# A graph network kernel: the opening stage's edge loads in rows of 112, 15 and 1, node scores laced with the normalisation, weight loads moved back

## What is computed

```python
h = jnp.maximum(_layernorm(x, axis=-1), 0.0)              # per node
hh = jnp.einsum('ni,hio->nho', h, W_att)
e = (hh[src] * a_src).sum(-1) + (hh[dst] * a_dst).sum(-1)  # 4 scores per edge
for _ in range(2):                                         # two hops of means
    h = segment_sum(h[src], dst) / deg
```

## Time and profile before

| what | us |
|---|---|
| median of 3 runs | 5965.78 |
| lowest and highest | 5952.73, 5968.33 |
| the profiled execution, its own time | 5961.54 |
| span of that execution | 5959.8 |
| busy: PE, DVE, POOL, ACT | 4565.7, 5147.9, 4326.5, 1746.8 |

### The profile page before, as it was taken

The page is one execution under the profiler, slowest core; times in us unless marked ns, Lnnn a source line. Parts: engine busy times, 40 slices in busy tenths (PEclk is TensorE's granted clock), DMA queues, the critical chain, the costliest instruction groups (busy, mean ns, idle before and its releaser), DMA issues. The chain is left out here.

```text
span 5959.8 us, 120870 instructions
## 1 busy us (share of the span) xinstructions
PE 4565.7 (77%) x44915; PEld 4261.9 (72%) x44915; DVE 5147.9 (86%) x13477; ACT 1746.8 (29%) x3789; POOL 4326.5 (73%) x4429
## 2 busy tenths in 40 slices
PE   5887773444434489999799997999979999799996
PEld 4776762222222379899799987999979999699996
DVE  6987776777777679999799997999979999799997
ACT  1111113767666522222122221222212222122221
POOL 4777778777777647777677776777767777677776
PEclk9999885665565689999799997999979999799998
DMA  3444443888888724444244442444424444344442
GB/s 90 123 117 117 117 111 109 299 292 293 291 290 291 249 75 117 116 114 116 74 118 114 117 113 76 117 114 115 116 73 119 115 116 114 80 112 115 115 116 79
DMA packets 514218, 827.78 MB, mean 139 GB/s; under 512 B 115666, under 2 KB 222043, under 8 KB 500577
## 3 DMA queue, kind: packets, MB, share of 16 engines
q1 hardware_dynamic: 372656, 645.16, 31.7%
q0 software_dynamic: 140976, 174.89, 16.4%
HBM read 385.20 MB, written 434.48 MB: 138 GB/s over the span
## 5 line engine op out<-in xcount | busy, mean ns | idle before, releaser
L663 POOL DMA_INDIRECT gring<-tableh,src_i x2778 | 2658.6, 957 | 997.3 <-issue 732.0
L1241 PE MATMUL psum<-penalty,arena 125*128 125x192 bf16 x25240 | 2309.1, 247 | 235.4 <-DVE es_w L1644 120.7
L1241 PEld LDWEIGHTS psum<-penalty,arena 125*128 125x128 bf16 x25240 | 2111.8, 98 | 277.8 <-issue 271.6
L663 POOL DMA_INDIRECT gring<-table,src_i x1414 | 1446.6, 1023 | 492.3 <-issue 406.3
L1644 DVE TENSOR_SCALAR arena<-dst_f,node_id 125x640 bf16<-125x640 f16 x5060 | 1746.6, 397 | 0.1
L898 ACT COPY run<-by_lane 128x512 f32<-128x512 f32 x505 | 570.1, 1129 | 2744.6 <-DVE by_lane L1706 2744.6
L1706 DVE TENSOR_TENSOR_SCAN by_lane<-mask_x,psum 128x256 f32<-128x256 f32 x1010 | 630.5, 663 | 0.2
L1579 DVE SCALAR_TENSOR_TENSOR arena<-arena,mask 128x324 f32<-128x324 f32 x808 | 444.3, 550 | 170.9 <-ACT arena L835 170.0
L1016 PE MATMUL psum<-ident,by_lane 128*128 128x128 f32 x202 | 66.6, 433 | 659.0 <-DMA by_lane<-attr_last 595.7
L1258 PEld LDWEIGHTS psum<-arena 128*128 128x128 f32 x4040 | 535.8, 193 | 14.4
L1016 PEld LDWEIGHTS psum<-ident,by_lane 128*128 128x128 f32 x202 | 29.2, 203 | 718.2 <-issue 718.2
(11 more groups left out here) (256 smaller groups left out, 4808.7 us busy)
## 6 DMA issues: line engine op xcount, KB each, us to landing
rows<-arena SPq DMA_DIRECT2D x101, 1296.0 KB, 5.1
acts<-arena SPq DMA_DIRECT2D x505, 256.0 KB, 2.1
arena<-acts SPq DMA_DIRECT2D x505, 256.0 KB
rowsg<-run SPq DMA_DIRECT2D x505, 256.0 KB
gring<-tableh,src_i POOLq DMA_INDIRECT x2778
rows<-run SPq DMA_DIRECT2D x101, 256.0 KB, 2.0
dst_f<-pe_src SPq DMA_DIRECT2D x253, 93.8 KB
gring<-table,src_i POOLq DMA_INDIRECT x1414
```

Source lines behind the costliest of these rows:

```text
L663: pool.indirect_dma_start(ring[:, s, k, :], None, table, bass.IndirectOffsetOnAxis(ap=src_i[:, c * K + k:c * K + k + 1], axis=0))\
L1241: ins = mm(found(n)[:, m, :], hot_at(n // 2, j)[:, at:at + P], parts[:, j, :, :].rearrange("q a f -> q (a f)"), start=(j == 0), stop=(j == ...
```

## The change

- The edge numbers are loaded as rows 0 to 111, rows 112 to 126 and the last row, three DMAs for each of `src_i` and `dst_i` (`edges_in` goes from 96 to 128).
- SP's fills of `ed_edges`, `rows*` and `attr_last` and its loads of `e1_hop`, `e1_gat` and `be1_c` move ahead of the table stores. The loads of `weights_in` move behind the first two `load_cols1` and `load_nat`.
- ACT laces the five square roots with the copies of the scores. The transposed group has two buffers (`hT2`: `hT` and the first 64 partitions of `yp`). PE transposes group g+1 ahead of the scores of group g; the transposes of `src_cols` stand before group 4's transposes.
- DVE's split of `t1` waits for the scores of its group instead of for the stored table, and the `pen_m` part stands between groups 3 and 4 of the split.
- The split of `be_rows` moves from ahead of chunk 0 into chunk 54; ACT doesn't wait for `weights_in` any more.
- `hT` is allocated ahead of `run1`, so the tiles between its two places lie at other addresses.

```diff
             for to, of in ((src_i, src), (dst_i, dst)):
-                sp.dma_start(to[0:P - 1, :], of[0:(P - 1) * T].rearrange("(p t) -> p t", p=P - 1))\
-                    .then_inc(edges_in, 16)
+                most = of[0:(P - 1) * T].rearrange("(p t) -> p t", p=P - 1)
+                for lo, hi in ((0, P - 16), (P - 16, P - 1)):
+                    sp.dma_start(to[lo:hi, :], most[lo:hi, :]).then_inc(edges_in, 16)
...
+        hT2 = (hT[:, :, :], yp[0:F, :, :])
...
+            ln_root(0)
             act.wait_ge(v_T, 1)
             copy(wattT[:, :, :], psum[0:F, 0, 0:H * F].rearrange("p (h i) -> p h i", h=H)).then_inc(v_Tsb, 1)
+            ln_root(1)
             act.wait_ge(v_ps, 1)
             copy(vvec[:, :], psum[0:F, 1, 0:2 * H]).then_inc(v_sb, 1)
+            copy_h0(0)
+            ln_root(2)
+            copy_h0(1)
+            ln_root(3)
+            copy_scores(0)
+            ln_root(4)
+            copy_h0(2)
+            copy_scores(1)
+            copy_h0(3)
+            copy_scores(2)
+            act.wait_ge(src_T_ps, 1)
...
+            copy_h0(4)
+            copy_scores(3)
+            copy_scores(4)
...
-            act.wait_ge(weights_in, N_WEIGHTS * 16)
...
             for g in range(NG):
-                if g == NG - 1:
+                if g == 3:
                     pe.wait_ge(src_cols_set, 1)
...
                 pe.wait_ge(h0_Tsb, g + 1)
+                if g + 1 < NG:
+                    pe.wait_ge(h0_ready, g + 2)
+                    transpose_group(t1[:, grp(g + 1), 0:F], 2, h0_T)
                 if g:
                     pe.wait_ge(es_sb, 2 * g)
                 for k in range(GJ):
-                    ins = mm(psum[0:NQ, 1, 64 + k * 2 * H:64 + (k + 1) * 2 * H], hT[:, k, :], vvec[:, :],
+                    ins = mm(psum[0:NQ, 1, 64 + k * 2 * H:64 + (k + 1) * 2 * H], hT2[g % 2][:, k, :], vvec[:, :],
                              start=True, stop=True)
                 ins.then_inc(es_ps, 1)
-                if g + 1 < NG:
-                    pe.wait_ge(h0_ready, g + 2)
-                    transpose_group(t1[:, grp(g + 1), 0:F], 2, h0_T)
...
+                    if k == 0 and c == 2 * NJ + 4:
+                        split_be()
...
-            dve.wait_ge(t1_out, NG * 16)
-            dve.wait_ge(t2h_ready, 1)
-            for g in range(NG):
+            def split1(g):
+
+                dve.wait_ge(es_sb, 2 * g + 2)
...
+            for g in range(NG - 1):
+                split1(g)
+            dve.wait_ge(bc_ready, 1)
...
+            split1(NG - 1)
+            dve.wait_ge(t1_out, NG * 16)
+            dve.wait_ge(t2h_ready, 1)
             dve.wait_ge(ed_zeroed, 96)
             dve.wait_ge(heads_set, 2)
             rows_from(0)
             rows_between(0)
             one_hot1(0, 0, NJ)
             one_hot1(1, 0, NJ // 2)
-            dve.wait_ge(weights_in, N_WEIGHTS * 16)
-            be = Steps(dve, be_steps)
...
```

More of the change, by code:

```diff
@@ L207, in part @@
             return stage[:, used[0] - width:used[0]]
+        hT = sb("hT", [F, GJ, NQ])
         act_in = part(SL * 4 * P).rearrange("p (s n) -> p s n", s=SL)
@@ L270, in build @@
         fold_b = sb("fold_b", [1, F])
-        hT = sb("hT", [F, GJ, NQ])
         xT = sb("xT", [P, 3, NQ])
@@ L454, in _ @@
             sp.dma_start(attr_last[0:LAST, :], attr[(P - 1) * T:E, :]).then_inc(attr_padded, 16)
[L456 to L469, removed]
             sp.wait_ge(e1_zero, 2)
@@ L480, in _ @@
                     sp.dma_start(be1_c[q * F:(q + 1) * F, :], be1.rearrange("l d -> d l")).then_inc(e1_in, 16)
+            for g in range(NG):
+                if g == NG - 1:
+                    sp.wait_ge(src_T_sb, 1)
+                    for i in range(3):
+                        rows = min(P, PE_COLS - i * P)
+                        sp.dma_start(pe_src[i * P:i * P + rows, :], src_T[0:rows, i, :]).then_inc(pe_src_out, 16)
+                sp.wait_ge(es_sb, 2 * g + 2)
+                sp.dma_start(node_rows(table1)[:, grp(g), :], t1[:, grp(g), :]).then_inc(t1_out, 16)
+            sp.dma_start(node_rows(ed_nodes), ed_sb[:, :, :]).then_inc(ed_out, 16)
             def store_acts(g):
@@ L519, in _ @@
             load_nat(1)
+            sp.dma_start(wg_sb[:, :], W_g).then_inc(weights_in, 16)
+            sp.dma_start(ww_sb[:, :, :], W_w.rearrange("(a f) o -> f a o", a=2)).then_inc(weights_in, 16)
+            sp.dma_start(bw_row[:, :], b_w.rearrange("(a f) -> a f", a=1)).then_inc(weights_in, 16)
+            sp.wait_ge(consts_set, N_CONSTS)
+            with nc.allow_non_contiguous_dma(reason="bias vector"):
+                sp.dma_start(bg_col[:, :], b_g.rearrange("(f a) -> f a", a=1)).then_inc(weights_in, 16)
+            for k in range(3):
+                sp.dma_start(be_rows[32 * k:32 * k + 1, :, :], be2.rearrange("(a l) f -> a l f", a=1)).then_inc(weights_in, 16)
+            sp.dma_start(b2_rows[:, :, :], b2.partition_broadcast(NQ)).then_inc(weights_in, 16)
+            sp.dma_start(lnp[:, :, 0:F], ln_g.partition_broadcast(NQ)).then_inc(weights_in, 16)
+            sp.dma_start(lnp[:, :, F:2 * F], ln_b.partition_broadcast(NQ)).then_inc(weights_in, 16)
+            with nc.allow_non_contiguous_dma(reason="one number per layer"):
+                sp.dma_start(lnp[:, :, 2 * F], dot_scale.partition_broadcast(NQ)).then_inc(weights_in, 16)
+                sp.dma_start(lnp[:, :, 2 * F + 1], res_w.partition_broadcast(NQ)).then_inc(weights_in, 16)
             for c in range(CH):
@@ L675, in _ @@
             pool.wait_ge(t1_out, NG * 16)
-            pool.wait_ge(edges_in, 96)
+            pool.wait_ge(edges_in, 128)
             settle()
@@ L729, in _ @@
                 gather_nodes(rowsg, agg_all, agg_in)
[L732 to L740, removed]
         @block.scalar
@@ L752, in _, with ln_root, copy_h0, copy_scores @@
             act.wait_ge(early_set, 2)
-            for g in range(NG):
+            def ln_root(g):
                 act.wait_ge(ln_var, g + 1)
                 ln_sqrt(g).then_inc(ln_std, 1)
+            def copy_h0(g):
+                act.wait_ge(h0_T, g + 1)
+                copy(hT2[g % 2], psum[0:F, 2:4, :].rearrange("p b n -> p (b n)")[:, 0:GJ * P]
+                     .rearrange("p (k n) -> p k n", n=P)[:, :, 0:NQ]).then_inc(h0_Tsb, 1)
+            def copy_scores(g):
+                act.wait_ge(es_ps, g + 1)
+                scores = psum[0:NQ, 1, 64:64 + GJ * 2 * H].rearrange("q (k h) -> q k h", k=GJ)
+                copy(t1[:, grp(g), F:F + H], scores[:, :, 0:H]).then_inc(es_sb, 1)
+                copy(ed_sb[:, grp(g), :], scores[:, :, H:2 * H]).then_inc(es_sb, 1)
+            ln_root(0)
             act.wait_ge(v_T, 1)
             copy(wattT[:, :, :], psum[0:F, 0, 0:H * F].rearrange("p (h i) -> p h i", h=H)).then_inc(v_Tsb, 1)
+            ln_root(1)
             act.wait_ge(v_ps, 1)
             copy(vvec[:, :], psum[0:F, 1, 0:2 * H]).then_inc(v_sb, 1)
[L761 to L766, removed]
+            copy_h0(0)
[9 more added lines that the diff above has]
+            act.wait_ge(src_T_ps, 1)
+            copy(src_T[:, 0:2, :], psum[:, 6, 0:2 * P].rearrange("p (i e) -> p i e", i=2))
+            copy(src_T[0:PE_COLS - 2 * P, 2, :], psum[0:PE_COLS - 2 * P, 6, 2 * P:3 * P]).then_inc(src_T_sb, 1)
+            copy_h0(4)
+            copy_scores(3)
+            copy_scores(4)
             copy(t2[:, :, F:2 * F], t1[:, :, 0:F]).then_inc(t2h_ready, 1)
-            act.wait_ge(weights_in, N_WEIGHTS * 16)
             act.wait_ge(consts_set, N_CONSTS)
@@ L1328, in _ @@
                 norm_relu(st, xin, g, t1, g, h0_ready)
-            dve.wait_ge(edges_in, 96)
+            dve.wait_ge(edges_in, 128)
             st.done(nc.vector.tensor_copy(src_cols[:, :].rearrange("p (c m) -> p c m", m=KMAX),
@@ L1354, in _ @@
             ts(diag[:, 1, :], ident[:, :], dst_f[:, 0:1], None, ALU.mult).then_inc(diag_ready, 1)
[L1355 to L1361, removed]
             def running_sums(to, c, rows, steps, n, between):
@@ L1440, in node_numbers, with split_be @@
                 nc.vector.tensor_copy(slot_i[0:NQ, :], tmpn).then_inc(slots_ready, 1)
+            def split_be():
+                dve.wait_ge(weights_in, N_WEIGHTS * 16)
+                be = Steps(dve, be_steps)
+                be.then(nc.vector.tensor_copy(be_tmp[:, :, :], be_rows[:, :, :]))
+                be.done(nc.vector.tensor_copy(be_parts[0:32, :, :], be_tmp[0:32, :, :]))
+                be.then(tt(be_rows[:, :, :], be_rows[:, :, :], be_tmp[:, :, :], ALU.subtract))
+                be.then(nc.vector.tensor_copy(be_tmp[:, :, :], be_rows[:, :, :]))
+                be.done(nc.vector.tensor_copy(be_parts[32:64, :, :], be_tmp[32:64, :, :]))
+                be.then(tt(be_parts[64:96, :, :], be_rows[64:96, :, :], be_tmp[64:96, :, :], ALU.subtract))
+                assert be.n == N_BE
             def hop_chunk(c):
@@ L1482, in _ @@
                 dve.wait_ge(parts1_ready, g + 1)
+            for g in range(NG - 1):
+                split1(g)
```

(10 more changed lines are left out.)

## The result

| | kernel before | changed kernel |
|---|---|---|
| median of 5 runs, us | 5965.78 | 5936.90 |
| lowest and highest | 5952.73, 5968.33 | 5934.64, 5942.29 |
| profiled execution, its span | 5959.8 | 5940.5 |
| ratio | | 0.9955, 95% interval 0.9942 to 0.9969 |

The changed kernel takes 28.9 us less by the medians, 18 to 35 us by the interval. The forecast was 5933 in a range of 5920 to 5952. The profiled executions differ by less, 19.3 us: that of before was 4.2 us under its kernel's median and that of the changed kernel 5.4 over its own.

The account below looks back on a forecast made before the run. POOL's gathers were taken to bound the hop stage from gather 1 on. An earlier start (12.7 us) plus the removed stall (18.6), less up to 1.6, gave 30.5 us: 5933 us, range 5920 to 5952.

Parts of the forecast that it names:

- What bounds it: Hop stage: its end is gather 1's start plus 606 POOL gathers plus POOL's stall on chunk 0; only first and last move.
- The edge numbers: Opening loads: split rows land near 18 us instead of 42.5, ahead of DVE's need at 22.9, 5 us to spare.
- The scores: ACT and PE opening: folding starts at 13.6, scores end at 35.3 instead of 48.0, gather 1 at 39.5; gain 12.7 us.
- SP's queue: Fills and biases ahead of the table stores end at 24, costing at most 1 us; weight loads, at most 15 us, hide.
- DVE and chunk 0: DVE opening: columns land at 43.2, 14.4 us to the first sum, chunk 0 starts at 57.6 instead of 94.6.
- The stall: POOL before gather 25: the 18.59 us stall goes, as chunk 0 ends at 64.2, 5.8 us before gather 25 is due.
- The sum: Start 12.7 plus stall 18.6 is 31.3, less up to 1.6 for first gathers beside busy DVE; 30.5 us taken.
- The first: Rival: edge numbers come no earlier (42.5), gather 1 at 55.0, stall still goes; gain 15.8, about 5949 us; 5%.
- The second: Rival: chunk 0 later than gather 25, costing one for one past 5.8 us; 15 us late gives 5943 us; 11%.
- The third: Rival: POOL's gathers slow beside busy DVE; 0.052 us more each eats the gain, 0.07 more gives 5975 us; 6%.
- The fifth: Rival: more gain, scores or landing faster by some us, 5925 us; 6%.
- The fourth: Rival: moved tiles change DVE's 635 one-hots by 10 ns each, 6 us gained to 6 lost; 0 in the sum.

Follow-up runs that it names:

- the second profile: The changed kernel itself, unchanged, run and profiled again on another chip: 5935.79 us against 5961.34 for the kernel before, ratio 0.9960.
- in two parts: Changed kernel with x and table stores as rows 0 to 111 and 112 to 124, plus one early square root on ACT: 5927.19 us, ratio 0.9943.
- roots first: Changed kernel with all five square roots ahead of the score copies on ACT, on a usual chip: 5940.67 us, gather 1 at 49.00.
- the kernel with the fills behind x: Changed kernel with SP waiting for x before the fills, but not before the edge numbers, on the slow chip: gather 1 at 39.97, no ratio.

## Why the prediction was right, point by point

- **What bounds it.** POOL from gather 1 to gather 606, and the stall on chunk 0. Right, and shown: holding chunk 0 back by 16.2 us gave a stall of 10.9 and 10.6 us at gather 606; by 5 us, no stall.
- **The edge numbers.** There at 22.9 without a wait: right, DVE took them at 24.62 as soon as it was free (x had made it 1.7 us later). The Trainium skill, DMA: Bandwidth & Descriptors, Rules for kernel authors, which holds such a split for useless, doesn't fit a load of 127 rows: here it did away with a wait of 19.6 us. The section of the Trainium skill, DMA: Bandwidth & Descriptors, on why a DMA increments its semaphore by 16 has the number of engines go by the divisors of the rows. That fits: the share was 0.06 with 127 rows and 0.97 with the split ones.
- **The scores.** Last store forecast at 35.3, measured 36.34. The folding started at 15.27 instead of 13.6, because x came 1.8 us later, a term the sum didn't have: the load that was made faster took from the load in front of it. The chain itself was right: from the start of folding to the last store 21.07, worked out 21.7. The 0.6 that it was faster lie between the end of group 0's scores and that of group 3's, 10.8 us instead of 11.4. The landing was taken as 4.2 and was 4.8. Gather 1 was 1.7 us late on the forecast (39.88 in the second profile).
- **SP's queue.** Fills and bias loads were through at 16.2, before 24: free, as said. The weight loads, at most 15 us, took 11.7, until 56.1, and the next columns' load stalled for 5 us behind them; it was covered.
- **DVE and chunk 0.** 57.6 forecast, 59.75 measured: x again, and 14.7 instead of 14.4 from one-hots to the first sum. That the split of `be_rows` gained nothing is in chunk 0's row: DVE waits 3.19 us for PE where it waited 2.21. The sum carried the 14.4 over from a place where POOL stood still for most of it. Now POOL gathers beside it, and the 37 one-hots take 11.5 us instead of 10.1 (last section); 0.3 of these 1.4 us reach chunk 0. Of the moves that made chunk 0 early, only the weights' was tried by itself: with them ahead it starts at 72.79 instead of 59.40. What the fills' and the split's are worth stays open.
- **The stall.** Gone, with a cover of 5.3 us against the 5.8 that were worked out.
- **The sum.** 12.7 + 18.6 less up to 1.6; measured 11.0 + 18.3 (the stall's row keeps the issue gap of 0.3), less 0.2 on the first 24 gathers (1.278 each against 1.269) and 2.1 on the other 581: 26.95. In the second profile the start gives 12.3 and gather 606 comes 31.4 sooner. The term that was mis-sized is the start, by x's landing. In the time, 30.5 us were forecast; the medians of the two pairs gave 28.9 and 25.6. That the first of them fell 4 us from 5933 says little by itself, as the attention stage alone wanders by 12 us between executions; it is the rows of the opening that bear the sum out.
- **The rivals.** The first was tried by itself and gained 11.6 us where 15.8 had been worked out, with its landing 2.6 us longer than the sum had it. The second was near: 5 us more and it begins. The third, a slower pace of the gathers, didn't show: their pace scattered without a sign of the change, and it was DVE's one-hots that got slower beside them; the second profile has 774.8 for 581 gathers against 775.5 before. The fifth didn't come either: the last store was 1.0 us late and landed 0.6 later than worked out. The fourth is out: one-hots to xin take 407 ns in both kernels, against the earlier trace rows:

```profile
L1671 DVE TENSOR_SCALAR xin<-dst_f,node_id 125x640 bf16<-125x640 f16 x635 | 228.3, 407 | 0.0
```

## What to carry to other kernels

Ask of every long wait in an opening stage what would be late next if it went: the 19.6 us on the edge numbers were worth nothing alone, and the reordering without them gave about half of the gain. Where one engine sets the pace from its first instruction on, only two things of the opening count, when it starts and whether its ring runs full, and DVE's 35 us of earlier start were worth the 18.3 that POOL had stalled. Look at the row count of a transfer before its size, and at what a faster transfer takes from the one that the path waits for.

## What the runs showed of the hardware

- A load of 127 rows moved at 25 GB/s; as 112, 15 and 1 rows, with no fills yet, the DMA engines were 0.97 busy at 243 GB/s from 6 to 9 us (the kernel with only the new load, above). In the changed kernel they were 0.99 busy at 366 GB/s from 9 to 14 us, with the edge numbers and the fills in flight:

```profile
9.00:14.00 5.00, 0.60 (x4) 0.39 (x4) 2.35 (x5) 0.64 (x1) 0.00 (x0) 1.00 0.99 366
```

- The same store of 166 KB took 3.1 (in two parts), 4.1 to 4.2, 4.8 and 6.8 us from its issue to POOL's start. The 6.8 stand behind the densest row of other stores, but 4.1 (roots first) and 4.8 (changed kernel) have the same issues ahead of them at the same distances, so what sets it stays open.
- DVE's one-hots paid for POOL's gathers. DVE's 37 one-hots ahead of chunk 0, in the kernel before (gathers beside only the first 2.4 us) and in the changed kernel (gathers beside all of them):

```profile
80.10:90.40 10.30, 10.14 (x37) 1.00 0.23 63
```
```profile
45.00:56.60 11.60, 11.52 (x37) 1.00 0.57 88
```

  In the timeline most follow each other by 0.26 us; one for each gather, 0.5 us into it, takes 0.47. So a gather costs DVE 0.2 us.
- On one chip the kernel before took 8271 us. In the four kernels profiled there TensorE stood idle 1 to 2.6 us ahead of single matmuls with no engine or DMA to wait for, and POOL waited over 1 us on the ring again and again, mostly at every second chunk. The granted clock of the kernel below was 1.00 up to 50 us and 0.76 from 50 to 100 us; the changed kernel on a usual chip has 1.00 in both stretches. From the timeline of PE there, the kernel with the fills behind x:

```profile
63.40 0.33 PE L1072 MATMUL psum<-x_nodes,arena 125*128 125x204 bf16 x1 [2.63 <-issue]
66.20 0.33 PE L1072 MATMUL psum<-x_nodes,arena 125*128 125x204 bf16 x1 [2.47 <-issue]
```

  What holds the instructions back there stays open. The opening up to gather 1 was as on the others.
